# Spiking recurrences in a 2048-token layer stack: each step's vector instructions split into two halves of the cells

## The reference, cut to what matters

```python
TAU_INV, V_TH, DECAY = 0.5, 1.0, 0.9
def lif_step(v, x_t):
    v = v + (x_t - v) * TAU_INV
    s = spike(v - V_TH)          # 1.0 where v >= V_TH
    v = v * (1.0 - s)
    return (v, s)
# R, K, V = x @ Wr.T, x @ Wk.T, x @ Wv.T; all three go through lif_step
h = h * DECAY + k * v
y = r * h
x1 = layernorm(residual + y @ Wo.T, ln1_g, ln1_b)
s1 = lif_scan(x1 @ W1.T + b1)            # 512 features
ffn_out = lif_scan(s1 @ W2.T + b2)       # 128 features
out = layernorm(x1 + ffn_out, ln2_g, ln2_b)
```

## The kernel before, in words

| call | cells | steps per pass | instructions of L1687 and L1688 in this run |
|---|---|---|---|
| `"rkv"` in `stage_l2_mix`, L1777 | 192 | 32 | 64 + 64 |
| `"hidden"` in `stage_l2_spikes`, L1900 | 128 | 64 | 108 + 108 |
| `"out"` in `stage_l2_spikes`, L1908 | 64 | 32 | 76 + 76 |

## Time and profile before

### The profile page before, as it was taken

How to read it: one execution, slowest core, us unless ns; L and a number is a source line. 1 busy time by engine, 2 the same in 40 slices (tenths; PEclk the granted TensorE clock), 3 DMA queues, 4 the chain that set the end, 5 groups by cost and what they waited for, 6 DMA issues and landing times. The chain is left out here.

```text
span 1930.1 us, 28529 instructions
## 1 busy us (share of the span) xinstructions
PE 1209.0 (63%) x10382; PEld 596.3 (31%) x10382; DVE 1332.2 (69%) x2971; ACT 830.0 (43%) x1538; POOL 266.0 (14%) x269
## 2 busy tenths in 40 slices
PE   6689999999999984669541630503026899321053
PEld 4112222222222233469431410301013557320043
DVE  3899999999999814554432248586877686667701
ACT  2159999999999973222100320300004366200021
POOL 2200000000000000132015240100033310100033
PEclk9579999999999996679855865756557879755577
DMA  2100100100010000000052310000003011200012
GB/s 64 44 7 22 30 21 19 28 25 18 24 30 18 3 2 13 18 1 1 1 166 91 95 33 0 1 0 0 0 18 126 24 45 30 91 0 1 2 48 60
DMA packets 50679, 58.87 MB, mean 30 GB/s; under 512 B 11832, under 2 KB 39483, under 8 KB 50268
## 3 DMA queue, kind: packets, MB, share of 16 engines
q1 hardware_dynamic: 45579, 49.78, 8.9%
q0 software_dynamic: 4224, 6.01, 1.2%
q10 hardware_dynamic: 736, 1.25, 0.2%
HBM read 30.17 MB, written 13.63 MB: 23 GB/s over the span
## 5 line engine op out<-in xcount | busy, mean ns | idle before, releaser
L622 ACT ACTIVATE l0att_probs<-l0att_ps_sv 128x512 f32<-128x512 f32 x1024 | 555.9, 595 | 84.2 <-PE l0att_ps_sv L592 72.5
L659 DVE TENSOR_REDUCE l0att_half_negmax<-l0att_ps_m 128x1 f32<-128x1024 f32 x480 | 547.1, 1214 | 6.0 <-PE l0att_ps_m L531 6.0
L561 PE MATMUL l0att_ps_sv<-l0att_probs,l_V_aug 128*32 128x256 f32 x4096 | 331.1, 392 | 5.3 <-ACT l0att_pv_sb L613 5.3
L592 PE MATMUL l0att_ps_sv<-l_Q,l_K 51*128 51x512 bf16 x1024 | 200.8, 389 | 2.5 <-ACT l0att_probs L622 0.2
L531 PE MATMUL l0att_ps_m<-l_K,l_Q 48*128 48x512 bf16 x960 | 186.0, 385 | 11.1 <-DVE l0att_half_negmax L659 7.1
L561 PEld LDWEIGHTS l0att_ps_sv<-l0att_probs,l_V_aug 128*32 128x32 f32 x4096 | 83.2, 108 | 199.2 <-issue 104.4
L257 PE MATMUL ada_ps<-ident_sb,xn 128*128 128x128 f32 x128 | 34.1, 457 | 138.4 <-DVE xn L250 138.4
L592 PEld LDWEIGHTS l0att_ps_sv<-l_Q,l_K 51*128 51x128 bf16 x1024 | 49.6, 93 | 216.6 <-ACT l0att_probs L622 204.0
L311 POOL CAST l0att_nm<-l0att_negmax 128x16 bf16<-128x16 f32 x16 | 3.2, 197 | 513.7 <-DVE l0att_negmax L635 513.7
L2586 PE MATMUL l3sel_ps_c<-l3sel_part,l3sel_ones 128*128 128x15 bf16 x56 | 10.8, 193 | 99.6 <-DVE l3sel_part L2611 99.6
L2775 ACT ACTIVATE l3mlp_rowsT<-l3mlp_ps_t,l3f_norm_l_lncols 128x512 f32<-128x512 f32 x4 | 3.1, 777 | 161.4 <-PE l3mlp_ps_t L2743 161.2
(11 more groups left out here) (563 smaller groups left out, 2284.2 us busy)
## 6 DMA issues: line engine op xcount, KB each, us to landing
l_Q<-l_qp SPq DMA_DIRECT2D x188, 32.0 KB
l_K<-l_kp SPq DMA_DIRECT2D x188, 32.0 KB
l3f_mlp_l_w<-in_l_w_dram SPq DMA_DIRECT2D x2, 2048.0 KB
l_sorted_in<-l1ffn_zeros SPq DMA_DIRECT2D x1, 3072.0 KB
l1exp_rows<-l_sorted_in SPq DMA_DIRECT2D x4, 768.0 KB, 4.7
l_sorted_out<-l1exp_y SPq DMA_DIRECT2D x4, 768.0 KB, 5.7
l_Q<-l_q_parts SPq DMA_DIRECT2D x18, 128.0 KB
l_K<-l_k_parts SPq DMA_DIRECT2D x18, 128.0 KB
```

The source lines that it names most:

```text
L561: mm = pe.matmul(ps_v[32 * c:32 * c + 32, cols], V_aug[:, kt, h, :], probs[:, kt % 2, c, cols], start=(kt == 0 and part == 0), stop=(kt == ...
L592: pe.matmul(ps_s[:, (n + i) % 3, :], K[at, h % HEAD_BUFS, c1(kt)], Q[at, h % HEAD_BUFS, c4(2 * pair + i)], start=True, stop=True).then_inc ...
L622: act.activation(probs[:, kt % 2, c, :], ps_s[:, n % 3, :], ACT.Exp).then_inc(expd, 1)
L659: dve.tensor_reduce(half_negmax[:, h % 2, t, half:half + 1], src, AX_X, ALU.max, negate=True).then_inc(m_read, 1)
```

## The change

`steps` no longer issues one instruction over all cells and waits for it. The cells are cut into two contiguous halves, and both halves of L1687's operation are issued, then both of L1688's. After each instruction the wait is for the instruction before it (`link.n - 1`), not for itself. At the end of a call of `steps` one `link.wait()` waits for the last. Nothing else is changed: what is computed, the passes and all other stages stay.

```diff
@@ -1680,12 +1680,21 @@
     by_group = lambda ap: ap.rearrange("p (g c) -> p g c", g=groups)
     unsettled = dve.alloc_register(f"{name}_unsettled")
 
+
+
+    halves = (slice(0, cells // 2), slice(cells // 2, cells))
+
     def steps(link, first, last):
 
         for t in range(first, last):
             before = v if t > 0 else shifted
-            link(dve.scalar_tensor_tensor(U[:, t], before, 0.5, X[:, t], ALU.mult, ALU.add))
-            link(dve.scalar_tensor_tensor(v, U[:, t], 1.0, U[:, t], ALU.is_lt, ALU.mult))
+            for half in halves:
+                link.mark(dve.scalar_tensor_tensor(U[:, t, half], before[:, half], 0.5, X[:, t, half], ALU.mult, ALU.add))
+                dve.wait_ge(m.step, link.n - 1)
+            for half in halves:
+                link.mark(dve.scalar_tensor_tensor(v[:, half], U[:, t, half], 1.0, U[:, t, half], ALU.is_lt, ALU.mult))
+                dve.wait_ge(m.step, link.n - 1)
+        link.wait()
 
     def hand_on(link):
         link(dve.tensor_copy(by_group(shifted)[:, :, 1:chunks], by_group(v)[:, :, 0:chunks - 1]))
```

## The result

| | before | changed |
|---|---|---|
| median of 4 runs | 1940.48 us (1933.98 to 1946.68) | 1909.65 us (1908.29 to 1910.07) |
| profiled execution, span | 1930.1 us | 1908.0 us |
| VectorE busy, instructions | 1332.2 us, 2971 | 1326.2 us, 3467 |

The ratio is 0.984, with a 95% interval of 0.9804 to 0.9877. The medians lie 30.8 us apart, the two profiled spans 22.1.

What follows compares the result with a forecast made beforehand. VectorE's dependent instructions in three recurrences were taken to bound the kernel. Savings of 5.5 + 9.0 + 5.1 less 1.0 and 0.2 made 18.4 us, moving the median from 1943.6 to 1925.2 us; range 1914 to 1950.

Steps and rivals of the forecast that it cites:

- What bounds the kernel: Three recurrences: only VectorE works there, so every microsecond saved in them is a microsecond of the end.
- The fixed part of 193 ns: Recurrences: each instruction waiting for its direct neighbour costs 193 ns besides its cells' time, 95.7 of 160.1 us.
- The two bounds: Period of a half: the larger of c + gap and (c + 193)/2, c its cells' time; 175, 142, 113 ns.
- The gap: Between overlapping neighbouring halves on VectorE: 75 ns besides the cells' time, taken from a possible 61 to 193.
- The ends of the calls: Nine calls of `steps`: each ends with a full wait after a half, giving 1.0 us back.
- The leftover wait: End of each call: second wait may be its own instruction, covered by the last half's 160 ns; 0.2 us in all.
- The rival of the smaller gap: Recurrences: overlap works with a gap of 65 ns instead of 75, saving 25 us, 1918 us; chance 0.12.
- The no-overlap rival: Recurrences: each half starts only when its neighbour is wholly through, 96 us more, 2039 us; chance 0.10.
- The rival of the handling on top of the gap: Recurrences: 34 ns of wait handling follow the gap; 209, 176, 142 ns a half, 1957 us; chance 0.13, wholly or partly.
- The rival of instructions supplied too slowly: Recurrences: 992 instructions, one every 113 to 175 ns, cannot be supplied fast enough; nothing measurable changes; chance 0.05.
- All other stages should keep their lengths within a microsecond: Outside the recurrences: no other stage was to change its length by more than a microsecond.

Runs made afterwards that it cites:

- the pairs: Changed kernel with no wait between the two halves and a full wait after each pair; one run of 1967.9 us.
- e3_full_wait: Changed kernel with each half waiting for its direct neighbour; one run of 2030.1 us.
- e6_relaxed: Changed kernel with both operations reading X alone and each wait for the instruction four places ahead; one run of 1915.2 us.
- e7_thirds: Changed kernel with three parts instead of two, each waiting for the instruction three places ahead; one run of 1943.7 us, kernel before beside it 1941.4.
- the second comparison: Kernel before and changed kernel, both unedited, timed again in five rounds on one chip; changed 1907.7 us beside 1932.2, ratio 0.9862.
- e8_out_whole: Changed kernel with the third recurrence (64 cells) in whole instructions with full waits; 1916.4 us, ratio to the kernel before 0.9865.

## Why the prediction missed, point by point

- **What bounds the kernel** was right: the recurrences' 22.3 us reached the end. From the start of the first recurrence to the end of the third the changed kernel is 22.0 us shorter, and layer 3's 2.6 come on top; from the start of the first recurrence to the end of the program it is 24.4; no other engine or transfer came into the recurrences.
- **The fixed part of 193 ns** for a dependent neighbour was right, for parts of every size: 293, 258 and 226 ns with full waits, for 293, 260 and 226.
- **The two bounds** were right in form. The third recurrence came out at the 113 ns of its wait, as forecast.
- **The gap** is the term of the sum that failed: "I take 75, since the row nearest in operation and the row nearest in shape and operands both lie there." It measured 69. Both rows that I took are of a first neighbour behind an instruction that had found the engine idle, and the pairs give 76 for just that. A recurrence is a running stream. The rows of running streams were in front of me, 61 and 65, and I set them aside by kind of operation, when what mattered was whether the engine was already running. The next line of the same timeline of the kernel before, a two-input instruction behind the pair that I took, had the stream's gap with such an operation: it starts 0.20 us after L1343, which is 133 of cells and 67 of gap. The term is 688 halves by 6 ns, 4.1 us: with the ends of the calls below, 22.3 in place of 18.4.

```profile
1409.92 2.28 DVE L1345 TENSOR_TENSOR l2add_tmp<-xn,l_add_l_ln2g 128x2048 f32<-128x2048 f32 x1
```

- **The ends of the calls**: full wait after the last half, 1.0 us forecast and 1.0 measured with one wait there. The leftover wait, put at 0.2 with "its cover is that half's 160 ns", costs 65 to 90 ns each, 0.6 to 0.7 us in all. It has no cover: the instruction that carries it runs only when the last half is done, and the follower comes after it.
- **The rival of the smaller gap** (65, saving 25) was nearer to the truth than the forecast and had a chance of 0.12. The no-overlap rival is what `e3_full_wait` measures, 2030 against its 2039, and is the price of the change without its waits. The rule that I quoted from the Trainium skill (page "VectorE: DVE Perf Modes", section "The DRAIN you can't avoid"), that the next instruction doesn't start before the pipe has emptied, so that only the number of operations matters, doesn't hold here: the same halves start 169 ns apart with the waits one place further off and 293 with full ones, at a recorded duration of 250. The same section adds that a next instruction which isn't held starts earlier; the 169 ns agree with that, and I left it out. The rival of the handling on top of the gap asked for 209 and 176 ns where the changed kernel shows 169 and 135.5, and `e6_relaxed` shows that no part of it is there. The rival of instructions supplied too slowly falls with the 91 ns of `e7_thirds`.
- **"All other stages should keep their lengths within a microsecond"** is the other step that failed, and it is why the time fell out of the range and not merely off the middle: with the recurrences' 22.3 us alone it would have been 1921. Layer 3's first two stages gave 2.6 us more; together that is 24.9, near the 24.5 of the second comparison. The other 6 of the first comparison's 30.8 were not traced to a stage, and their cause stays open; the kernel before's own runs were spread over 12.7 us, its median was 1940.5, 1932.2 and 1941.4 us in three comparisons, and two stages ahead of the change spread by 4.9 and 8.9 us in the profiles. A range for a difference of medians of so few runs has to hold that, and mine, counted from 1943.6, held 6 us of it.

## What to carry to other kernels

In a chain of dependent VectorE instructions on one buffer, cut the work into two independent parts and let each instruction wait only for the one it needs, two places ahead. Here it paid because twice the gap (2 x 69) is less than the fixed part of a dependent start (193), so with two parts and not with three, and not at all with full waits. Put no second wait on the instruction behind such a chain. To price an overlap from a trace, take the period inside a run of queued instructions, not the distance of two neighbours behind a wait.

## What the runs showed of the hardware that I had not expected

- The gap between overlapping SCALAR_TENSOR_TENSOR instructions is 76 ns behind one that found VectorE idle and 69 in a stream. The recorded duration in a stream is no measure of either: with 96 cells its median was 250, 240 and 258 ns in the changed kernel's two profiles and in that of `e8_out_whole`, with starts 169 ns apart in all three.
- A second wait ahead of one instruction becomes an instruction of its own; it runs when the awaited half is done and the follower starts 64 to 72 ns behind it, 65 to 90 ns later than with one wait.
- Layer 3's first stages, with the same 340 matmuls, take 93.2 us or 88.3 though nothing in them is changed, and they are long where TensorE was long at 1.2 GHz in them (30.7 us of 93.2, 26.8 of 90.6, 27.3 of 90.4, 17.7 of 88.3). A pad of 4.6 us in front of them cost nothing. The stretch between the first two recurrences moves likewise: 52.5 us in both kernels, 54.0 to 54.7 in four of the variants.
